# Attention averages with the values stationary, in four lanes of 32 rows, and the loop unrolled by two

## What is computed

```python
num[t] = sum over s <= t of (q[t] . k[s]) * v[s]
den[t] = sum over s <= t of (q[t] . k[s])
att[t] = num[t] / (den[t] + eps)
```

## Time and profile before

| what | value |
| --- | --- |
| median of 3 runs | 733.06 us (731.43 to 738.74) |
| the profiled execution, its time | 734.74 us |
| the profiled execution, first to last instruction | 733.0 us |
| mean granted clock of TensorE | 0.953 |
| attention block, first instruction to the experts' first | 68.9 to 398.1 us |

### The profile page before, as it was taken

The page is one execution under the profiler, slowest core; times in us unless marked ns, Lnnn a source line. Parts: engine busy times, 40 slices in busy tenths (PEclk is TensorE's granted clock), DMA queues, the critical chain, the costliest instruction groups (busy, mean ns, idle before and its releaser), DMA issues. The chain is left out here.

```text
span 733.0 us, 17468 instructions
## 1 busy us (share of the span) xinstructions
PE 663.8 (91%) x4943; PEld 609.1 (83%) x4944; DVE 508.2 (69%) x1508; ACT 439.7 (60%) x867; POOL 450.1 (61%) x478
## 2 busy tenths in 40 slices
PE   3687999999999999999963899999999999998993
PEld 2556588888888888888961699999999999998993
DVE  3124358888888888888844479988889868865651
ACT  1022677766666666667611477777767767765771
POOL 7773334666666666666544447677776757857844
PEclk9789999999999999999975799999999999999998
DMA  8317122323333333332010424333353364463423
GB/s 177 88 20 223 50 72 80 80 80 79 79 79 79 79 79 79 79 79 70 26 53 4 100 30 63 62 56 58 67 66 65 56 127 57 74 127 54 68 37 32
DMA packets 63364, 53.77 MB, mean 73 GB/s; under 512 B 25318, under 2 KB 57722, under 8 KB 63322
## 3 DMA queue, kind: packets, MB, share of 16 engines
q0 software_dynamic: 19168, 23.48, 19.2%
q1 hardware_dynamic: 44154, 29.84, 16.6%
HBM read 29.72 MB, written 21.99 MB: 71 GB/s over the span
## 5 line engine op out<-in xcount | busy, mean ns | idle before, releaser
L1290 POOL DMA_INDIRECT result<-e_y,e_tag x78 | 130.8, 1676 | 83.1 <-DVE e_y L1594 42.2
L1337 PE MATMUL e_yp<-x_w2s,e_hh 128*128 x468 | 140.1, 367 | 3.7 <-DVE e_y L1594 2.0
L1586 DVE TENSOR_TENSOR e_hl<-e_hid,e_hh 128x512 fp32r<-128x512 f32 x117 | 80.4, 689 | 62.4 <-ACT e_hh L1398 61.5
L533 POOL DMA_INDIRECT tbl_dram<-c_entry,a_slot x64 | 64.5, 1008 | 87.8 <-DVE c_entry L1097 62.0
L1390 ACT ACTIVATE e_hid<-e_hidden,e_b 128x256 f32<-128x256 f32 x234 | 102.4, 474 | 26.5 <-PE e_hidden L1324 8.7
L1338 PE MATMUL e_yp<-x_w2s,e_hl 128*128 x468 | 117.9, 252 | 0.0
L1398 ACT CAST e_hh<-e_hid 128x512 fp32r<-128x512 f32 x117 | 72.5, 621 | 64.6 <-PE e_yp L1338 64.6
L629 PEld LDWEIGHTS a_ab<-a_values,a_masked 128*128 128x128 f32 x768 | 94.5, 191 | 13.4 <-issue 11.5
L629 PE MATMUL a_ab<-a_values,a_masked 128*128 (+1 forms) x768 | 100.1, 271 | 3.3 <-DVE a_masked L953 3.1
L1263 POOL DMA_INDIRECT e_x<-x_dram,e_tag x78 | 83.2, 1066 | 28.9 <-issue 22.6
L1337 PEld LDWEIGHTS e_yp<-x_w2s,e_hh 128*128 128x128 f32 x468 | 88.9, 190 | 4.6 <-issue 4.6
(11 more groups left out here) (251 smaller groups left out, 1562.9 us busy)
## 6 DMA issues: line engine op xcount, KB each, us to landing
a_raw<-in_ew SPq DMA_DIRECT2D x16, 288.0 KB, 3.1
h_dram<-x_w2s SPq DMA_DIRECT2D x8, 384.0 KB, 3.4
c_hb<-h_dram SPq DMA_DIRECT2D x16, 192.0 KB
a_raw<-in_ew SPq DMA_DIRECT2D x16, 192.0 KB, 2.6
a_raw<-in_ew SPq DMA_DIRECT2D x32, 96.0 KB, 2.6
result<-c_hb SPq DMA_DIRECT2D x16, 192.0 KB
x_dram<-a_xn SPq DMA_DIRECT2D x16, 192.0 KB
result<-e_room POOLq DMA_DIRECT2D x4, 768.0 KB, 8.8
```

The costliest lines, as they stand in the source:

```text
L1290: pool.indirect_dma_start(out=out, in_=y[:, i % YR, j], in_offset=None, out_offset=bass.IndirectOffsetOnAxis(ap=tag[:, i % TR, j, 0:1].bit ...
L1337: pe.matmul(Y[:, j, 0:2 * D], hh[:, f, c], w(f, 2 * D), start=f == 0, stop=False, skip_group_check=True)
L1586: g.tensor_tensor(hl[:, f:f + 2].rearrange("p f t -> p (f t)"), hid[:, f:f + 2].rearrange("p f t -> p (f t)"), hh[:, f:f + 2].rearrange("p ...
```

## The change

- In `average` the values are the weights, 17 columns, and the 128 masked columns of the head move. Head r of a group of four writes PSUM partitions 32r to 32r+16 (a lane), group g the columns 128g to 128g+127. `AB` now holds one half j at a time, with the tokens along the columns.
- `average_before` has the state as weights, padded to 32 columns a head, and the turned query features moving: four matmuls with 128, 64, 64 and 128 weight columns, the two of 64 in different halves of the partitions.
- `lanes_out(j)` is new on ACT: it copies a half's sums, 128x384, to SBUF. The first is placed after `features(0)` and ahead of the copy of the turned xn2; the second after `keys_out(1)`. `average_before` waits for the first, since it reuses `AB`.
- `turn_lanes` is new on PE, six 128x128 transposes at the end of each iteration into `FB` (the last time `FA`). It waits for both copies and for `keys_out(1)`. `normalise` reads its result and waits for it.
- On PE the order changes. Before: score 0, score 1, turn_att, average 0, prefix, turn of xn, score 2, project, qk 0, v, average_before, qk 1, average 1, turn_second, average 2, score 3, gate, score 4, score 5, average 3. After: score 0, score 1, prefix, turn of xn, turn_att, average 0, score 2, project, qk 0, v, qk 1, average 1, average 2, score 3, turn_second, score 4, gate, score 5, average_before, average 3. The rest stays, with the turn of the lanes behind it. ACT copies xn ahead of the attention. DVE's order is the same.
- The loop body holds two iterations and runs over 4 to 13; the buffer of the values is chosen when the program is written (`odd`), not by a register.
- The table's rows lie in `feat[0]`, and so POOL clears them after its last scatter. POOL clears `state` at the start, DVE clears `AB`. SP's waits ahead of `load_h` get an instruction of their own.

```diff
+LANE = 32
-        values = sb("values", [P, 2, TJ * H + 1, VW])
+        values = sb("values", [P, 2, TJ * H, VW])
-        state = sb("state", [CF, 2, CV])
+        state = sb("state", [CF, 2, HC, LANE])
+        lanes = [att[:].rearrange("p j d -> p (j d)"), sb("lanes", [P, NG * P])[:]]
-        sheet = sb("sheet", [1, 448])
+        sheet = feat[0][0:1].rearrange("p h f -> p (h f)")
...
+            for i in range(4):
+                emit(i, True, i >= 1, i >= 2, i >= 3, i % 2)
+            with eng.Fori(4, B - 2, 2) as i:
+                for odd in range(2):
+                    emit(i + odd, True, True, True, True, odd)
+            for i in range(B - 2, B + 3):
+                emit(i, i < B, i <= B, i <= B + 1, True, i % 2)
...
@@ gpsimd
-            g.memset(values[:, :, TJ * H:], 0.0).then_inc(s["setup"], 1)
+            pool.wait_ge(s["setup"], 1)
+            g.memset(state[:], 0.0).then_inc(s["setup"], 1)
...
-            for n in range(3):
-                g.memset(sums[n], 0.0).then_inc(s["table_set"], 1)
-            g.iota(tile_no, ...)
...
             sched(pool, emit)
+            pool.wait_ge(s["state_done"], B)
+            for n in range(3):
+                g.memset(sums[n], 0.0).then_inc(s["table_set"], 1)
+            g.iota(tile_no, ...)
             pool.wait_ge(s["scattered"], 16 * 4 * B)
...
@@ tensor: average_before, average, turn_lanes
-                    for c in range(2):
-                        pe.matmul(AB[:, 2 * P + c * CV:2 * P + (c + 1) * CV], qf_t[:, c], state[:, c],
-                                  start=False, stop=False, skip_group_check=True)
+                    pe.wait_ge(s["lanes_out"], 2 * b + 1)
+                    for c, h, n, row, g in ((0, 0, 4, 0, 0), (0, 4, 2, 0, 1), (1, 0, 2, 2 * LANE, 1), (1, 2, 4, 0, 2)):
+                        pe.matmul(AB[row:row + n * LANE, g * P:(g + 1) * P],
+                                  state[:, c, h:h + n].rearrange("p h v -> p (h v)"), qf_t[:, c],
+                                  start=g == 0, stop=False, skip_group_check=True)
...
-                            pe.wait_ge(s["att_ready"], i - 1)
+                            pe.wait_ge(s["lanes_out"], 2 * b)
...
-                        last = pe.matmul(beside(o + r * VW), masked[n % 2][:, r],
-                                         own_and_zeros.unsqueeze(1).broadcast_to([P, 2, 2, VW]),
-                                         start=n == 0 and r == 0, stop=True, skip_group_check=True)
+                        last = pe.matmul(AB[r * LANE:r * LANE + VW, g * P:(g + 1) * P],
+                                         values[:, 1 - odd, j * H + g * GH + r], masked[n % 2][:, r],
+                                         start=j == 0, stop=True, skip_group_check=True)
...
+                def turn_lanes(to):
+                    for j in range(TJ):
+                        pe.wait_ge(s["lanes_out"], 2 * b + j + 1)
+                        for g in range(NG):
+                            last = pe.transpose(to[:, j * 4 * P + g * P:j * 4 * P + (g + 1) * P],
+                                                lanes[j][:, g * P:(g + 1) * P], ident[:])
+                    last.then_inc(s["lanesT_done"], 1)
...
@@ tensor: the end of an iteration
+                if two:
+                    pe.wait_ge(s["kT_out"], TJ * (i + 1))
+                    turn_lanes(FB)
...
@@ scalar
+                def lanes_out(j):
+                    act.wait_ge(s["av_done"], 6 * b + NG * (j + 1))
+                    if j == 0 and (not fixed(i) or i >= 2):
+                        act.wait_ge(s["attT_done"], b)
+                    act.copy(lanes[j], AB[:, 0:NG * P]).then_inc(s["lanes_out"], 1)
...
                     features(0)
+                if two:
+                    lanes_out(0)
+                if fixed(i) and i == B:
+                    lanes_out(1)
                 if tail:
                     act.wait_ge(s["xn2T_done"], i - 1)
...
                     keys_out(1)
+                if one and two:
+                    lanes_out(1)
...
@@ vector
+            v.memset(AB[:], 0.0).then_inc(s["cleared"], 1)
...
-                ab = AB[:].rearrange(...)[:, :, 0:H * VW]...
+                turned = FA if fixed(b) and b == B - 1 else FB
+                ab = turned[:].rearrange(...)[:, :, 0:H * LANE]...
-                dve.wait_ge(s["av_done"], 6 * (b + 1))
+                dve.wait_ge(s["lanesT_done"], b + 1)
...
-                if not fixed(b) or b >= 1:
-                    dve.wait_ge(s["attT_done"], b)
```

More of the change, by code:

```diff
@@ L410, in attention_block @@
         ex_i, row_i = keep["ex_i"], keep["row_i"]
-        sheet = sb("sheet", [1, 448])
+        sheet = feat[0][0:1].rearrange("p h f -> p (h f)")
         PAD = NE // 2
-        table = [sheet[:, 32 * n:32 * n + NE] for n in range(4)]
+        table = [sheet[:, NE * n:NE * (n + 1)] for n in range(4)]
         n_of, tiles_i, tiles_f, jump = table[0], table[1].bitcast(I32), table[2], table[3]
-        sums = [sheet[:, 128 + 32 * n:128 + 32 * n + PAD + NE] for n in range(4)]
-        tile_no, ex_f, row_f = (sheet[:, 256 + 64 * n:256 + 64 * n + NTILE] for n in range(3))
+        sums = [sheet[:, 32 + 12 * n:32 + 12 * n + PAD + NE] for n in range(4)]
+        tile_no, ex_f, row_f = (sheet[:, 80 + 40 * n:80 + 40 * n + NTILE] for n in range(3))
         slot, slot_f = sb("slot", [P, 2, TJ], U32), sb("slot_f", [P, 2, TJ])
@@ L536, in store_slots, with emit @@
                     ).then_inc(s["scattered"], 16)
-            def emit(i, one, two, tail, choice):
+            def emit(i, one, two, tail, choice, odd):
                 unit = lambda w: w[:, bass.ds(i, 1)].rearrange("k u f -> k (u f)")
@@ L577, in _ @@
             pe.wait_ge(s["setup"], 5)
-            pe.wait_ge(s["cleared"], 1)
+            pe.wait_ge(s["cleared"], 2)
             def idle(n):
@@ L729, in emit @@
                     score(1)
-                if tail:
-                    turn_att()
-                if two:
-                    average(0)
                 if choice:
@@ L760, in emit @@
                     last.then_inc(s["v_done"], 1)
-                if two:
-                    average_before()
                 if one:
@@ L766, in emit @@
                     average(1)
+                    average(2)
+                    score(3)
                 if tail:
@@ L769, in emit @@
                 if two:
-                    average(2)
-                    score(3)
+                    score(4)
                 if tail:
@@ L774, in emit @@
                 if two:
-                    score(4)
                     score(5)
+                    average_before()
                     average(3)
```

74 lines of the change are left out of this document (30 added, 44 removed).

## The result

| | before | after |
| --- | --- | --- |
| median | 735.9 us | 815.9 us |
| ratio, 95% interval | | 1.0985 (1.0815 to 1.1155) |
| profiled execution, span | 733.0 us | 811.2 us |
| mean granted clock of TensorE | 0.953 | 0.873 |

What follows compares the result with a forecast made beforehand. PE was taken to bound the attention loop, busy 198.7 of 201.9 us. Terms of +0.4 (start), +1.2 (iterations 1 and 2), 18.9 (13 periods), +1.5 (last pass) and +2.3 (table) made +24.3, giving 757 us, range 733 to 772.

Steps and rivals of the forecast that it cites:

- the layout: One attention iteration laid out anew from the old trace's rows, with three new waits in PE's in-order stream.
- 13 x 1.45 = 18.9: Attention loop: 13 full periods, each taken as 1.45 us longer than 18.32 us.
- PE's busy share would fall from 98% to 82%: Attention loop: sign expected in the profile after, PE's busy share down from 98% to about 82%.
- three rivals: Waits do not hold PE, 697 to 724, 0.12; about even, 733 to 741, 0.13; lanes don't overlap, 782, 0.07.
- start, to the first T0: Before the loop's first key turn (T0): POOL clears state ahead of PE's first work, +0.4 us.
- iterations 1 and 2: First attention iterations: no prefix yet, but already the turns and, in 2, the gate's wait, +1.2 us.
- last passes and table: After the loop: normalise waits for copy and turns, +1.5 us; table memsets move behind POOL's last scatter, +2.3 us.
- The period: Attention loop, one iteration from first key turn to the next: 19.5 to 20.1 us instead of 18.32.
- the loop's form: Unrolling the loop moves only address arithmetic of PE's sequencer: put at nothing, 0.1 us either way.
- Prefix behind the state: Early in an iteration PE stands before prefix until DVE's state copy is out, some 1.8 us.
- gate behind ACT's two copies: Later in an iteration gate waits for ACT's first lanes copy, then xn2's: some 1.1 us of wait.
- Slower: Whole kernel slower by over 1%, that is over 740.4 us: chance 0.76.

Runs made afterwards that it cites:

- e12: Kernel before, no lanes, with ScalarE copying the turned xn five times and xn2 three times, so TensorE waits more: 886.9 us.
- e1: Changed kernel with unused matmuls in both waits, eight ahead of prefix and four ahead of gate: 772.4 us, ratio 1.051.
- e14: Kernel before with only the loop's new form, two iterations to a pass, no lanes and no order changed: ratio 1.0006.
- e9: Changed kernel with DVE's copy of the state issued ahead of normalise, at the end of an iteration: 770.2 us.
- e11: e10 with the table's scratch row in a tile of its own, set early as in the kernel before: 766.8 us, ratio 1.034.
- e10: e9 with ACT's first copy of the lanes moved behind that of xn2: 759.6 us, ratio 1.033.
- e18: Kernel before with 26 unused matmuls in TensorE's waits of its last passes: ratio 1.0024.
- e3: Changed kernel with only the four unused matmuls ahead of gate, none ahead of prefix: 780.5 us.
- e15: e13 with gate put back ahead of score 5: 752.8 us, ratio 1.026.
- e8: Kernel before, no lanes, with only PE's order at the iteration start and ACT's order of two copies from the change: 749.3 us.
- e4: Changed kernel with both waits filled as in e1, each filler with 17 weight columns in place of 128: 772.6 us.
- e17: Kernel before, no lanes, with ScalarE copying the turned xn three times and xn2 twice: 760.8 us.
- e7: Changed kernel with ACT's first lanes copy behind that of xn2 and prefix behind turn_att and average 0: 755.9 us, ratio 1.023.
- e13: e11 with PE reordered to cover three remaining waits, score 5 ahead of gate: ratio 1.072, on a chip where before took 780 us.

## Why the prediction missed

**What failed.** For the greater part not a step of the layout but a term that the sum did not have: the cost of a fallen clock, 45 us over the 13 periods. The rest of the miss is the layout's own term, 18.9 us forecast and 26.5 measured, and the last passes. The sum took every new wait at its own length, "13 x 1.45 = 18.9", as if durations stayed those of a loop at clock 1.00. The prediction itself said that PE's busy share would fall from 98% to 82%, and did not ask what that does to the clock. The trace of before had rows for the question: in its last passes the clock falls at 374.2, right behind a wait of 1.21 us (the row at 373.78 above), and gate takes 1.78 us instead of 0.98. The Trainium skill, "TensorE: Matmul & The Clock Gate", section "A second HAM failure mode: psum-queue depth-cycling", tells of a kernel in which short idle times between groups of matmuls were frequent enough to make the clock swing between its two levels; after and e12 agree, with mean clocks of 0.81 and 0.72 in their loops. None of the three rivals had it.

**The terms**, from the profiled executions. The first T0 is at 84.1 and 85.4, the last at 357.3 and 430.6, the experts' first matmul at 398.16 and 477.47:

| term | forecast | measured |
| --- | --- | --- |
| start, to the first T0 | +0.4 | +1.3 |
| iterations 1 and 2 | +1.2 | +0.3 |
| 13 periods, layout | +18.9 | +26.5 (by e1, at full clock) |
| 13 periods, fallen clock | not in the sum | +45.3 |
| last passes and table | +3.8 | +5.9 |
| experts | 0 | -1.1 |
| sum | +24.3 | +78.2 |

The first row is no measure of the forecast's +0.4: e1, with the same start, has its first T0 at 83.7, ahead of before's.

**The layout.** The period was forecast at 19.5 to 20.1, 19.77 in the sum. It is 19.96 in the written-out iterations, which makes 2.5 of the 7.6 us by which 26.5 is over 18.9. Passes inside the loop are some 0.4 us longer than the written-out ones (e1: 20.33 to 20.59 against 19.96; before: 18.33 against 18.12), above the forecast's range, and this makes the other 5.1. In every second pass the first mask starts 0.27 us later; in the others it does not, but the residual add behind the projection does, by 0.28. The sum took the loop's form for free. By e14 it is free in the kernel before; why it costs more with lanes was not settled.

**The waits.** Prefix behind the state (1.80 forecast and measured) and gate behind ACT's two copies (1.1 forecast, 0.67 measured at full clock, 0.97 beside a fall) hold. e9 shows the first by its cause: the state's copy moved ahead, the wait ahead of prefix is gone.

**The last passes and the table.** This is the end of after on PE, to be read against before's rows of the count and the experts above, with the start of DVE's table behind it; then the end of e11, with the early table:

```profile
465.36 0.22 PE L824 MATMUL a_fa<-count,c_ones 128*128 128x8 bf16 x2 [0.34 <-DVE count L1095]
477.47 0.37 PE L1311 MATMUL e_yp<-ident,pot 128*32 128x128 f32 x1 [11.90 <-PEq L369]
...
472.75 0.15 DVE L1125 COPY a_feat<-a_fa 1x8 f32<-1x8 f32 x1 [5.87 <-POOL a_feat L564]
```

```profile
428.03 0.22 PE L823 MATMUL a_fa<-count,c_ones 128*128 128x8 bf16 x2 [0.34 <-DVE count L1094]
438.54 0.37 PE L1310 MATMUL e_yp<-ident,pot 128*32 128x128 f32 x1 [10.29 <-PEq L369]
```

From the count to the experts it is 12.1 us against 10.0, so +2.1 for the table where +2.3 was forecast; in e11 it is 10.5, 1.6 less than in e10, where 2 to 3 were expected. The stretch is no constant, though: in e18 it is 12.6 with the early table. The last passes cost +3.9 instead of +1.5: in after the clock is at its lower level for 38 of the 45 us from 438 on. The mechanism of the table is the one forecast: before, its chain ran beside POOL's last scatters, now it starts behind them.

**The chances.** Slower had 0.76, rightly. The range held the layout's error and nothing of the clock: even the run with the clock held is at 772.4, just past its upper end.

## What stays open

How much idle time it takes. More idle PE, made by more copies on ScalarE, brings the clock down in the kernel before (e12), and work in the waits holds it in after (e1), but the amount of idle time does not order the runs. With lanes, e3 stands idle for 2.4 us of a full-clock period and falls in 2 of 13, e15 for about 1.2 us and falls in 7. e8, without lanes, stands idle for 1.15 us and never falls. So the lanes, or the six turns that came with them, may count for less than full-width work and have a part in it, and the place of a wait may matter; no run here separates these. e4 speaks only of long fillers with few weight columns. Nor is it shown that the copies themselves have no part in e12. Open too is why e17 has one fall of 27.3 us in iterations 1 and 2 and none later.

## To carry over

When a change puts new waits in front of an engine that was busy all the time, read its granted clock as a term of the sum: here a layout 26 us longer cost 45 more in clock, and filling its waits with useless matmuls gave some 40 back. Look in the old trace for a stretch where the engine already waits as it will, and take the durations from there. Price a saving on the bounding engine only after asking what each in-order queue does with the new order: moving one 0.36 us copy on DVE (e9) took some 40 us off, more than the 1.1 us a period by which the lanes cut PE's work.

## What the runs showed of the hardware

- Four lanes of 17 columns in four column groups, float32, overlap in after: the four of a pass start within 0.02 us, and the next pass starts 0.11 to 0.12 behind.
- Narrow fillers (17 weight columns) held the clock as well as full-width ones: 772.6 and 772.4 us.
- Where the clock falls in some iterations only, executions of one kernel differ by more than those of one that holds it: e7 had 747.0 to 760.1 us in four, e1 771.8 to 773.4.
- On one chip (e13, e14) the clock was at 0.50 for 65 and 68 us near the start, the first T0 came 43 us later, and the kernel before took 780 us instead of 735.
